# A six-part macaron network (FFN, scan attention, MoE, Mamba) in fp32: the Mamba sum over states by accumulating transposes, with new order tables

## What is computed

```python
x = x + 0.5 * _L0_ffn_ref(_layernorm(x), ...)     # ternary weights, gelu, inner layer norm
x = x + _L0_attn_ref(_layernorm(x), ...)          # selective scan over 16 states, gelu gate
x = x + 0.5 * _L0_ffn_ref(_layernorm(x), ...)
x = x + 0.5 * _L1_ffn_ref(_layernorm(x), ...)     # sigmoid encode, top-2 of 8 experts, decode, layer norm
x = x + _L1_attn_ref(_layernorm(x), ...)          # Mamba: conv, silu, scan over 16 states, gate
x = x + 0.5 * _L1_ffn_ref(_layernorm(x), ...)
```

```python
dA = exp(delta[b,l,d] * A[d,n]);  dBu = delta * Bm[b,l,n] * u
carry = dA * carry + dBu          # state per channel and n, along the tokens, in chunks of 32
y[b,l,d] = sum_n carry[d,n] * Cm[b,l,n]
y = y * silu(res);  out = y @ W_out.T + b_out
```

## Time and profile before

| what | us |
|---|---|
| median of 3 runs | 1116.94 (1114.31 to 1121.48) |
| span of the profiled execution, first to last instruction | 1116.6 |
| time of the profiled execution outside its span | not given apart; the median lies 0.3 above the span |
| part before the first scan half reaches PE | 171 |
| part with the scan (256 halves) | 884 |
| part after the scan | 62 |

### The profile page before, as it was taken

The page is one execution under the profiler, slowest core; times in us unless marked ns, Lnnn a source line. Parts: engine busy times, 40 slices in busy tenths (PEclk is TensorE's granted clock), DMA queues, the critical chain, the costliest instruction groups (busy, mean ns, idle before and its releaser), DMA issues.

```text
span 1116.6 us, 11275 instructions
## 1 busy us (share of the span) xinstructions
PE 935.0 (84%) x3446; PEld 451.9 (40%) x3446; DVE 762.5 (68%) x1717; ACT 659.4 (59%) x1030; POOL 515.7 (46%) x413
## 2 busy tenths in 40 slices
PE   6457888799889979998999799969996898689865
PEld 4234344344434434444444344434433343343332
DVE  3213417983898388878896699748974959499921
ACT  4344557576657765796668855866585424644221
POOL 2131227462745365556454654555454616555311
PEclk9668999999989989999999999989998899889986
DMA  3002017441735263456252744255434525374320
GB/s 136 10 1 86 1 54 249 143 132 48 246 120 164 73 229 130 167 158 210 86 181 96 227 180 163 92 172 208 142 123 136 202 108 206 119 270 134 142 86 9
DMA packets 44717, 151.83 MB, mean 136 GB/s; under 512 B 4464, under 2 KB 12784, under 8 KB 40560
## 3 DMA queue, kind: packets, MB, share of 16 engines
q1 hardware_dynamic: 44656, 151.11, 39.5%
HBM read 148.21 MB, written 2.88 MB: 135 GB/s over the span
## 4 chain that ended last, share of the span: by engine, by line
PE 46%; DVE 25%; ACT 14%; issue 6%; POOL 6%; DMA 2%; SPq 0%; DVEq 0%; POOLq 0%; ACTq 0%
DVE dA L982 11%; PE yp L1483 9%; ACT L116 5%; PE mp L1442 5%; PE pp L1362 4%; PE mp L1427 3%; PE fp L1264 3%; PE fp L1248 3%; PE pp L1228 3%; DVE hs L989 3%; ACT dA L1207 2%; PE mp L1451 2%; POOL dbu L708 2%; PE mp L1228 2%; PE pp L1332 1%
## 5 line engine op out<-in xcount | busy, mean ns | idle before, releaser
L708 POOL TENSOR_TENSOR dbu<-du,b_row 128x1024 f32<-128x1024 f32 x128 | 301.2, 2356 | 178.8 <-DVE dA L982 176.9
L982 DVE TENSOR_TENSOR_SCAN dA<-dA,dbu 128x512 f32<-128x512 f32 x256 | 312.4, 1220 | 75.5 <-ACT dA L1207 41.5
L1483 PE MATMUL yp<-hs,ident 128*128 128x512 f32 x512 | 273.1, 636 | 58.2 <-DVE hs L989 57.7
L1207 ACT ACTIVATE dA<-delta,pr 128x512 f32<-128x512 f32 x256 | 173.8, 686 | 104.3 <-DVE hs L989 103.1
L989 DVE TENSOR_TENSOR hs<-dA,c_row 128x512 f32<-128x512 f32 x256 | 177.0, 691 | 28.1 <-PE yp L1483 18.2
L116 ACT ACT_TABLE_LOAD x130 | 166.8, 1283 | 15.0 <-POOL delta L639 11.4
L1483 PEld LDWEIGHTS yp<-hs,ident 128*128 128x128 f32 x512 | 89.7, 196 | 169.4 <-DVE hs L989 101.7
L1427 PE MATMUL mp<-cont,ex_ 64*128 64x512 f32 x128 | 75.5, 671 | 15.5 <-DVE he L940 11.6
L1431 PE MATMUL mp<-cont,ex_ 64*128 64x512 f32 x128 | 75.6, 672 | 3.2 <-DVE he L945 3.2
L1248 PE MATMUL fp<-sq,w 128*128 128x512 f32 x128 | 71.1, 679 | 5.7 <-ACT sq L1030 4.1
L1264 PEld LDWEIGHTS fp<-w,hT 128*128 128x128 f32 x512 | 63.5, 193 | 29.2 <-issue 14.1
(11 more groups left out here) (219 smaller groups left out, 1426.9 us busy)
## 6 DMA issues: line engine op xcount, KB each, us to landing
b_row<-held SPq DMA_DIRECT2D x104, 512.0 KB, 4.9
c_row<-held SPq DMA_DIRECT2D x104, 512.0 KB, 4.1
gsp<-gheld SPq DMA_DIRECT2D x32, 1024.0 KB, 6.6
xin<-L_attn_x SPq DMA_DIRECT2D x8, 256.0 KB, 3.0
out<-xb SPq DMA_DIRECT2D x8, 256.0 KB, 2.3
ex_<-c_ex SPq DMA_DIRECT2D x1, 1001.0 KB, 8.0
b_row<-c_ps SPq DMA_DIRECT2D x1, 768.0 KB, 9.4
pr<-c_pr SPq DMA_DIRECT2D x1, 567.0 KB, 10.4
```

Source lines behind the costliest of these rows:

```text
L708: pool.tensor_tensor(out=dbu[:, j % 2, :].rearrange("p (r t) -> p r t", r=2), in0=d, in1=b_n, op=ALU.mult).then_inc(dbu_r.sem, 1)
L982: dve.tensor_tensor_scan(out=dA[:, half], data0=dA[:, half], data1=dbu[:, j % 2, half], initial=0.0, op0=ALU.mult, op1=ALU.add).then_inc(h ...
L1207: act.activation(out=dA[:, r * SEQ:(r + 1) * SEQ], in_=delta[:, i % 2, c, :], func=ACT.Exp, scale=mA[:, c, 2 * k + r:2 * k + r + 1]).then_ ...
L1483: pe.matmul(yp[:, :], lhsT=ident[:, :], rhs=hs[:, j % 2, r * SEQ:(r + 1) * SEQ], start=(s % PAIRS == 0 and r == 0), stop=(s % PAIRS == PAI ...
```

## The change

The sum over the states is made in transposed form. For each half, four `is_transpose` matmuls (128x128, `hs` stationary, the identity moving) accumulate into `yp`, so `yp` holds y with tokens in the partitions. When the 16 halves of a channel group are in, ACT copies `yp` to a new SBUF tile `ys` and PE turns it back with four more transposes into `yp`; DVE then multiplies by the gate as before. These are a new thread Y on ACT, PE and DVE. On POOL, the back half of MoE waits for its own previous addition before it writes `dg` again. All five order strings are written anew; fillers K go from 44 to 7. The diff, cut:

```diff
@@ ORDER @@
     "PE":
-        "PFEPFEFFFFFFFFFFFFFFFFFFFFFFFFPFPFFPFFPFPEFFPPPKKKKEKFEFEEEFEFEKKFFKFPFPFFFPFFPPPKPFPFKKFFSSKPSFSFPS"
+        "PFFFFFFFFFFFFEFFFKPFKFFFFFFFFFFPFPFFPFFEPFPFFPEPEEPFFEEEFFEEFFFFFFFPFPFPPPPPFPFFFSFFSPFPSFPFSPSSPSES"
...
@@ POOL, back(m) @@
                 pool.wait_ge(ddr.sem, ddr.at(m, 1))
+                if m >= 1:
+                    kind, before = M_TURNS[m - 1]
+                    last = hx_new if kind == "moef" else xo_new
+                    pool.wait_ge(last.sem, last.at(before, 1))
...
@@ DVE, s_thread @@
-                        if s % PAIRS == PAIRS - 1:
-                            yield True
-                            dve.wait_ge(sum_ps.sem, h + 1)
-                            dve.wait_ge(min_r.sem, min_r.at(i, 2 * IC))
-                            if i >= 1 and c == 0:
-                                dve.wait_ge(mo_ps.sem, mo_ps.at(i - 1, 1))
-                            dve.tensor_tensor(out=yg[:, c, :], in0=yp[:, :], in1=g4[:, i % 2, c, :],
-                                              op=ALU.mult).then_inc(yg_r.sem, 1)
...
+            def y_thread():
+                for i in range(BATCH):
+                    for c in range(IC):
+                        yield True
+                        dve.wait_ge(yt_ps.sem, yt_ps.at(i, c + 1))
+                        dve.wait_ge(min_r.sem, min_r.at(i, 2 * IC))
+                        if i >= 1 and c == 0:
+                            dve.wait_ge(mo_ps.sem, mo_ps.at(i - 1, 1))
+                        dve.tensor_tensor(out=yg[:, c, :], in0=yp[:, :], in1=g4[:, i % 2, c, :],
+                                          op=ALU.mult).then_inc(yg_r.sem, 1)
...
@@ ACT @@
+            def y_thread():
+                for i in range(BATCH):
+                    for c in range(IC):
+                        yield True
+                        act.wait_ge(sum_ps.sem, 2 * (i * STEPS + (c + 1) * PAIRS))
+                        if i or c:
+                            act.wait_ge(yt_ps.sem, yt_ps.at(i, c))
+                        act.activation(out=ys[:, :], in_=yp[:, :], func=ACT.Copy).then_inc(ysum_r.sem, 1)
...
@@ PE, s_thread @@
-                            pe.matmul(yp[:, :], lhsT=ident[:, :], rhs=hs[:, j % 2, r * SEQ:(r + 1) * SEQ],
-                                      start=(s % PAIRS == 0 and r == 0), stop=(s % PAIRS == PAIRS - 1 and r == 1)
-                                      ).then_inc(sum_ps.sem, 1)
+                            first, final = s % PAIRS == 0 and r == 0, s % PAIRS == PAIRS - 1 and r == 1
+                            for q in range(TILES):
+                                at = r * SEQ + q * P
+                                last = pe.matmul(yp[:, q * P:(q + 1) * P], lhsT=hs[:, j % 2, at:at + P],
+                                                 rhs=ident[:, :], is_transpose=True, start=(first and q == 0),
+                                                 stop=(final and q == TILES - 1), skip_group_check=True)
+                            last.then_inc(sum_ps.sem, 1)
+
+            def y_thread():
+                for i in range(BATCH):
+                    for c in range(IC):
+                        yield True
+                        pe.wait_ge(ysum_r.sem, ysum_r.at(i, c + 1))
+                        for q in range(TILES):
+                            last = pe.transpose(yp[:, q * P:(q + 1) * P], in_=ys[:, q * P:(q + 1) * P],
+                                                identity=ident[:, :])
+                        last.then_inc(yt_ps.sem, 1)
```

More of the change, by code:

```diff
@@ L62 @@
[L62 to L70 removed]
+        "FFFPFEFFFEFFFFFFPPPFFFPEEEEEEEEFFFEPFFFPSSSSSSSSFSFFPPSSSSSSSEESFEESEYEFEFESSSSSESSPSSSSFFSFSSYPSSSS"
@@ new lines @@
+        "FSFFSSSPSSPSFSFFSSEESSEESEESEYSESSSSESPSPSSSSFSFFPSSYSSFSSFFSPPPSSSSSSEESPEEFPSESFEEFSESSSPSESYEEPEE"
+        "EESSSESESSSSFFFPSSSSESSYSSSSPPPSSSFSFFEESSEEPSEEESPESSFSFFSEESEPYEPESEESSSSSSEEFSSFSPFSSSESSYSSSSSPP"
+        "PSSFSSSSFSFEPEPSEESESEPESFESFFYSESEESPEEEEESSESSSSSSFSFFPSYESSSSSSPPSSPSSFSSFEFEEPESSEEPSESEFSSFFSYE"
+        "EEPSPSEESEESSESESSSSSFFSSPSSYSESSSPPPSSSSSSEESSEESSPEEPESESSYSSESEPEPEESEESSESPESSSESSSSSSYSSSPPSSSP"
+        "PSSSSSSSSSESEEPPEYESEESSESSSSSSEESSEESESEEYEEPPPPEEEEEEEEEE",
@@ new lines @@
+    "ACT":
+        "FFFFFFPFFFFFFFFFFFFFFFFFFFPFPFFPFFFPFPFPPPFFFFFEEEFFFEFFFFFPFPPPPPFPPPFFFSSFFSSPFSFPSFSSPPSPPSSFPFSS"
+        "SFSSFSFSSYSFSESEESFSSFFEFFSFFSSFSPPSSPSPFPFPFFPPYPFFSFSPFPSFPSSSPSFSPFSFSPSFFPSSSFSFSFSSFYFSFSSESFSE"
+        "ESFSESFSSPSPSPSSPFPFPFFPPYPFFFFSFSPSPSPSPPFPFSPSPSPSFPSPSSFPSPFSSPSSFEFSEESYSFFFEFSFSPFPSFSSSPSEPSSP"
+        "EEPSPPFPSSFPSSFPFFYFSSPFPSSPFSPEFPSPSPSPPPSSFSFSFSPFSPSFESEEFYSSFESFFFPFSFSPSFSPSFPSSPSPSSPEPFPESFES"
+        "PSFPFYFFSFSPFSSPSPSFPSPPSPSSEPSSPPSSFPFFPSFSYSFESSEEFFSFFEFFPSSSPSFFSPSFESSPEPPSSEPPPFYFFSPSPSSPFPSP"
+        "SFFPSSFFPSSFSPSPPPPSFESFSPSFFFPSSYESEESFFSFEFFFSPSPFSFPSPSSPPESPSEFSSPPSSEYSSPSPPSPSPSSPPPSSPSPSPSSS"
+        "SPYPSPSSEESSEESSEPPSSPSPSPEPSEPSESPPSSPSPYSPSPSSPESSPSPSSSSSPSPSSPSPSSSPYPSPSSSESSESESSSSSEYPPPPPPEP"
+        "EEEEEEE",
@@ L428, in build @@
         hs = sb("hs", [P, 2, 2 * SEQ])
+        ys = sb("ys", [P, SEQ])
         yg = sb("yg", [P, IC, SEQ])
@@ L436, in build @@
         sum_ps = signal("sum_ps", STEPS)
+        ysum_r = signal("ysum_r", IC)
+        yt_ps = signal("yt_ps", IC)
         yg_r = signal("yg_r", IC)
@@ L1490, in k_thread @@
                     yield True
-                    alone = order[:at].count("S") in (0, 2 * BATCH * STEPS)
+                    alone = order[:at].count("S") == 0
                     pe.matmul(yp[:, 0:FILL], lhsT=zeros[:, :], rhs=w1[:, 0:FILL], start=alone, stop=alone,
                               skip_group_check=True)
-            side_by_side(ORDER["PE"], F=f_thread(), P=p_thread(), E=e_thread(), S=s_thread(), K=k_thread())
+            side_by_side(ORDER["PE"], F=f_thread(), P=p_thread(), E=e_thread(), S=s_thread(), Y=y_thread(),
+                         K=k_thread())
 def stacked(*parts):
```

40 lines of the change are left out of this document (15 added, 25 removed).

## The result

The changed kernel takes 1091.1 us (median of 4 runs, 1089.2 to 1094.15), the kernel before 1119.0 beside it (1114.3 to 1121.5): a ratio of 0.976, with a 95% interval from 0.972 to 0.980. It is faster by 28 us at the medians where the forecast was 58. The sign is right and the time lies in the range; the step that sized the gain is not right.

A forecast was written before the change was run, and what follows sets the result against it. No engine alone was the bound; PE's queue, holding DVE up some 96 us, was the largest cause of lost time. Waits summed to -59, checks gave -50 and -66; -58 was taken from 1116.6, giving 1059, range 1018 to 1112.

The forecast's parts named there:

- The sums' length: On PE, each of 256 sums was to take 0.43 us instead of 0.87, 113 us less work.
- Turning back: Per channel group: 6.9 us more on PE, 9.5 on ACT; 5 us added on the path to `yg`, 19 uncovered.
- Fillers: Middle part: 23 fewer fillers, 15 us less on PE; their price might be below nothing, through the clock.
- Table loads and POOL's new wait: ACT: 130 loads become 119, 14.1 us less, net 4.6, 3 counted; POOL's wait for its own addition costs nothing.
- The ledger of DVE's idle time: Middle part: DVE's waits for PE and ACT were to shrink by 59 us in all, as PE's work fell 121.
- `hs`: forecast -14: DVE's 18.2 us wait for a free `hs` buffer was to lose three quarters, with half the sum's length.
- `yg`: forecast -27: DVE's 31.9 us wait of `yg` for the sum was to go, less 5 us added for turning back.
- In the others I let 15 go: DVE's four other rows of waits for PE, 46.3 us, were to lose about a third with PE's backlog.
- Both checks: Whole kernel by the last-ending chain: -50 us; middle part at DVE's best window share, 85%: 818 us, -66.
- DVE's work "the same": On DVE, the change was to leave the amount of work and the busy time unchanged.
- rival 1: PE's clock in the middle part falls to 0.78, transposes holding it no better than pauses: 1136 us; chance 0.11.
- Rival 2: DVE's waits for PE turn into waits for ACT and POOL, hiding the gain: about 1114 us; chance 0.09.

The follow-up runs named there:

- the filled kernel: The changed kernel with 219 more fillers (matmuls of zeros) in idle places of PE's list: 1078.7 us, ratio 0.963 to the kernel before.
- the kernel of its own: A separate test kernel, computing nothing of the network: transposes, sums and fillers for PE's clock, small DVE operations alone and beside POOL's products; no overall time given.

## Why the forecast was half right

- **The sums' length: right.** 1024 records. In PE's timeline of the kernel after, 12 transposes reach from 531.59 to 532.95, 0.45 us per four:

```profile
531.59 1.53 PE L1506 MATMUL yp<-ident,hs 128*128 128x128 f32 x12
532.95 0.60 PE L1254 MATMUL fp<-ident,hT 128*128 128x128 f32 x4
```

- **Turning back: right in its work** (9.5 us of copies on ACT as counted). No run shows the 5 us on the path: leaving it all out of the filled kernel gained nothing.
- **Fillers: not borne out.** I credited the absence of 23 of them with 15 us on PE and left the clock to a rival. No run puts just these back; filling the idle places with 219 gains 1.3%, which fits the price below nothing that the term named.
- **Table loads and POOL's new wait: right in number** (119; DVE's wait for POOL fell). The 3 us from ACT did not come; DVE's wait for ACT rose by 5.
- **The ledger of DVE's idle time: this step failed.** It took each wait released by PE for backlog that shrinks with PE's load. The two longest, 17.4 and 17.6 of 96.4 us, are waits for a chain at the change of sequence, and the short sums alone left both as they were. I had read the 17.4 as "PE's alone". `hs`: forecast -14, came -7. `yg`: forecast -27 to some 5 us; it is at 26.8 in its two rows, -5, and 17.8 of that are the same two places. In the others I let 15 go and 15 went, but by other ways: `fs` lost 24, of which 13 now stand in the rows of `yg` and `dbu` at the same place, and `he` gained 13, which the order alone brings. With ACT's 8 missing, DVE's 17 more work and POOL's 16 less the account closes: 59 - 22 - 7 - 8 - 17 + 16 = 21, and the middle part lost 20. Both checks, by the chain and by the best window, shared the flaw: they gave the freed time to the end, though its place can be taken by whatever stands in the list.
- **DVE's work "the same": wrong by 17 us.** The same instructions, 14 of the 17 us in two small ones that now run beside POOL's products. This term I did not have; taking it away gained 1.7%.
- **The clock: the direction of rival 1, not its mechanism or size.** It fell to 0.90, not below 0.80. Filling the idle places, with the transposes as they are, brings it back to 0.96, so idle time and not the transposes let it fall. PE's busy time is 878 us and not 810, because matmuls that nobody touched left longer records (the experts' two lines 23 us more). Part of that is the order's: with it alone PE is busy 948.8 us, 14 more than before, though 37 fillers (25 us) are gone.
- **Rival 2** (the gain is hidden) names what held for the short sums alone, but the waits that held it were PE's list and its chain, not new waits for ACT.

The parts as ratios: order alone +0.35%, short sums alone (without turning back) -0.7%, both -2.4%. The gain is in the pair: the order was made for short sums. With both hidden costs removed the kernel takes 1057.8, near my 1059, but that confirms nothing of the ledger: it is another kernel, and there the sums' work is no longer what is waited for.

Still open: how much of DVE's 45 us for ACT's exponential a further order could remove, whether the fillers' whole gain runs through the clock, and why the experts' matmul takes longer in the new order at nearly the same mean clock. No run tried any of them.

## What to carry to other kernels

Before a wait "for PE" is credited to a shorter instruction, look at what stands ahead of that instruction in its engine's list and what that waits for; a wait that ends with the next stage's input is a chain: a shorter instruction left it as it was here, and only the order shortened it. Compare such waits by place, since the row they are booked to can change. A form and an order that come together should be run apart, since here neither is worth much without the other. When TensorE gets emptier, price what its idle time does to its clock, and when an order changes, look for small operations whose mean has jumped.

## What the runs showed of the hardware

- A DVE operation of 8 or 32 numbers per partition that reads and writes SBUF alone can wait out a whole two-input product of POOL: 2.11 us instead of 0.16 (copy, 2.19 in the kernel of its own) and 2.21 instead of 0.19. With an operand in PSUM it runs beside it (0.167, 0.196, and 0.72 for a 128x512 product). The Trainium skill ("GPSIMD Engine Reference", 1. Specifications) says that POOL shares its SBUF interfaces with DVE, with contention for instructions with two SBUF inputs or in a 2-port mode. The traces agree that there is contention: here the small operation ended with POOL's product (423.65 and 423.62). Which of the two conditions the copy meets no run shows.
- fp32 transposes hold the upper clock, 1.00 at eight per 1.45 us and in 320 in a row (0.109 us each by the stretch of 35 us), and accumulating ones cost no more (0.45 us per four).
- Matmuls of zeros in idle places raised the clock from 172 to 1000 us from 0.90 to 0.96 and gained 1.3% in the new order. With the short sums in the old order they raised it over the span from 0.875 to 0.922, and gained nothing that the intervals can tell.
